# A Hyena block with a gated feed-forward on one core: three steps moved in ScalarE's instruction list

## What is computed

```python
u  = x @ in_proj_w.T + in_proj_b                  # 512 -> 3*512
uc = depthwise causal conv of 3 taps over u + short_b
x0, x1, v = split(uc)
v  = v * x1
v  = fftconv(v, k, filter_bias)                   # k: a 512-tap filter from a small sine network
y  = v * x0
x  = layernorm(x + y @ out_proj_w.T + out_proj_b)
gate = silu(x @ Wg.T); up = x @ Wu.T              # 512 -> 1408, quantised weights
x  = layernorm(x + (gate * up) @ Wd.T)
```

## Time and profile before

| | us |
|---|---|
| median of 3 runs | 1137.11 |
| lowest, highest | 1135.48, 1208.80 |
| the profiled execution, its own time | 1135.29 |
| its span, first to last instruction | 1133.5 |
| TensorE matmul busy | 1042.8 |
| VectorE, GpSimd, ScalarE busy | 794.9, 631.5, 463.3 |

### The profile page before, as it was taken

One profiled execution on the slowest core, in us unless ns is written; L12 is line 12 of the kernel. 1 busy time (PEld: TensorE's weight loads), 2 busy tenths in 40 slices (PEclk: granted clock), 3 DMA queues, 4 the chain that ended last, 5 costly groups with the idle time before them and its releaser, 6 DMA issues.

```text
span 1133.5 us, 18043 instructions
## 1 busy us (share of the span) xinstructions
PE 1042.8 (92%) x6378; PEld 839.7 (74%) x6378; DVE 794.9 (70%) x1455; ACT 463.3 (41%) x995; POOL 631.5 (56%) x677
## 2 busy tenths in 40 slices
PE   5896759999999999999999999999999999978996
PEld 3565647787887888788887888788887878867774
DVE  5666646687776878677787868677787878685443
ACT  3355524344444343444444444434444444423242
POOL 0147656557474657557475667557474657575211
PEclk9797979999999999999999999999999999999998
DMA  5245330222122221222222221222121221312332
GB/s 163 61 159 170 127 121 19 66 85 75 57 75 85 65 69 44 84 85 75 56 76 89 67 69 38 84 85 75 56 76 51 67 71 38 94 47 94 109 86 84
DMA packets 52215, 90.58 MB, mean 80 GB/s; under 512 B 6362, under 2 KB 11098, under 8 KB 52126
## 3 DMA queue, kind: packets, MB, share of 16 engines
q1 hardware_dynamic: 49072, 85.25, 24.8%
q10 hardware_dynamic: 3054, 4.18, 1.1%
HBM read 78.14 MB, written 11.27 MB: 79 GB/s over the span
## 4 chain that ended last, share of the span: by engine, by line
PE 73%; DVE 12%; ACT 5%; issue 5%; POOL 2%; DMA 2%; ACTq 0%; POOLq 0%; DVEq 0%
PE gate_up L884 10%; PE gate_up L885 10%; PE bank L756 10%; PE bank L758 10%; PE bank L757 10%; PE down L895 6%; PE down L896 6%; PE bank L847 2%; DVE hid_lo L746 2%; ACT hid L527 2%; DVE tmp L676 2%; PE spectrum L756 1%; PE spectrum L758 1%; PE spectrum L757 1%; PE bank L869 1%
## 5 line engine op out<-in xcount | busy, mean ns | idle before, releaser
L557 POOL TENSOR_TENSOR acc<-acc,tmp 128x256 f32<-128x256 f32 x160 | 124.3, 777 | 131.9 <-DVE tmp L676 121.2
L676 DVE TENSOR_TENSOR tmp<-spectrum,filt 128x512 f32<-128x512 f32 x256 | 173.1, 680 | 0.0
L756 PE MATMUL bank<-xT_hi,win_hi 128*128 128x512 f32 x384 | 162.9, 424 | 10.2 <-DVE cv L652 5.3
L884 PE MATMUL gate_up<-x2T_hi,wg_sb 128*128 128x256 f16 x704 | 167.4, 278 | 0.0
L885 PE MATMUL gate_up<-x2T_lo,wg_sb 128*128 128x256 f16 x704 | 165.4, 275 | 0.0
L884 PE MATMUL gate_up<-x2T_hi,wu_sb 128*128 128x256 f16 x704 | 163.7, 273 | 0.0
L885 PE MATMUL gate_up<-x2T_lo,wu_sb 128*128 128x256 f16 x704 | 163.5, 273 | 0.0
L895 PE MATMUL down<-wd_sb,hid_hi 128*128 128x512 f32 x352 | 148.9, 423 | 10.0 <-DVE hid_lo L746 5.3
L758 PE MATMUL bank<-xT_hi,win_lo 128*128 128x512 f32 x384 | 155.9, 406 | 0.0
L757 PE MATMUL bank<-xT_lo,win_hi 128*128 128x512 f32 x384 | 155.6, 405 | 0.0
L740 DVE SCALAR_TENSOR_TENSOR hid<-gate_up,up_scale,hid 128x256 f32<-128x256 f32 x176 | 84.5, 480 | 89.4 <-ACT hid L527 88.8
(11 more groups left out here) (110 smaller groups left out, 2161.1 us busy)
## 6 DMA issues: line engine op xcount, KB each, us to landing
wd_sb<-wd_scratch SPq DMA_DIRECT2D x176, 256.0 KB, 2.6
xstage<-in_x SPq DMA_DIRECT2D x32, 256.0 KB, 4.4
x<-in_x SPq DMA_DIRECT2D x32, 256.0 KB, 2.8
out<-x SPq DMA_DIRECT2D x32, 256.0 KB, 3.2
x<-in_win SPq DMA_DIRECT2D x12, 256.0 KB, 3.0
x2T_lo<-in_wd SPq DMA_DIRECT2D x6, 256.0 KB, 2.8
wd_scratch<-x2T_lo ACTq DMA_DIRECT2D x6, 256.0 KB, 2.1
x<-in_wd SPq DMA_DIRECT2D x5, 256.0 KB, 2.8
```

The source lines that it names most:

```text
L557: G.tensor_tensor(acc[:, i, 0, :], acc[:, i, 0, :], t[:, 1, :], ALU.subtract)
L676: TT(dst, spectrum[j % 2][:, :, :], k_part, ALU.mult).then_inc(made_done, 1)
L756: mm(out_ap, ah, bh, start=k == 0, stop=False)
L884: mm(dst, w[:, kb, rows(q)], x2T_hi[:, kb, ts], start=kb == 0, stop=False)
```

## The change

Three steps change their place in the list. The reader of `iv` is now called `y` and holds VectorE's three operations alone, at the old place. A step `z` with ScalarE's high part and GpSimd's low part stands right behind `silu` of the same beat. `norm` of the first layer norm moves from the tail of beat 9 to beat 10, behind `gu` and ahead of all other steps there. `psplit` of sum 3 moves from the tail of beat 9 to the tail of beat 10, behind `xsplit`.

```diff
-READER = {"ip": "conv", "iv": "z", "op": "ln1", "tv": "vsplit", "xt": "xsplit", "x2t": "x2split"}
+READER = {"ip": "conv", "iv": "y", "op": "ln1", "tv": "vsplit", "xt": "xsplit", "x2t": "x2split"}
@@ beat_steps
     earlier = shared(n, beat - 1) if beat else shared(n - 1, HB - 1)
+    if beat == 10 and out:
+        steps += [("norm", LN1, n - 2)]
     steps += readers([p for p in earlier if p[0] not in ("xt", "x2t")])
...
     if u:
         steps += [("silu", *u)]
+    steps += [("z", *at) for kind, *at in earlier if kind == "iv"]
...
-    if beat == 9 and out:
-        steps += [("norm", LN1, n - 2)]
     if beat in (9, 10):
         steps += readers([p for p in shared(n, beat) if p[0] == "xt"])
-    for i, ready in enumerate((1, 4, 7, 9)):
+    for i, ready in enumerate((1, 4, 7, 10)):
@@ build, VectorE's list
-                elif kind == "z":
+                elif kind == "y":
```

## The result

| | before | changed |
|---|---|---|
| median of the runs, us | 1137.8 | 1117.4 |
| lowest to highest | 1135.5 to 1208.8 | 1116.8 to 1119.1 |
| the profiled execution, its own time | 1135.3 | 1119.1 |
| its span | 1133.5 | 1117.3 |

The ratio is 0.9831 with a 95% interval of 0.9814 to 0.9849 (one disturbed run of before, the 1208.8, is left out of it): 1.7% less, just short of 2%, and 1115 had been forecast in a range of 1109 to 1123. The difference of the two medians is 20.4 us; by the ratio the saving is 19 us. The diff adds one line ahead of the engines' code, so L870 of the changed kernel is L869 of before, L641 is L640, and so on. The instructions are the same 18043.

A forecast was written before the change was run, and what follows sets the result against it. TensorE was taken as the bound from 200 to 990 us. Terms 10.8 + 5.2 + 1.2 + 3.2 = 20.4 us, off the profiled execution's 1135.3, gave 1114.9, said as 1115; range 1109 to 1123.

The forecast's parts named there:

- What bounds: From 200 to 990 us TensorE bounds; two of its waits, at transposes and down projection, carry 16.9 of 18.7 idle us.
- Activation before z, beat 9: Beat 9's product, high and low part come 0.95 us earlier; the even stages' down projection stalls go, 5.2 us.
- norm behind xsplit: Odd stages: the transposes' stall of 2.35 us goes, 0.56 returns at x2t; net 1.8 us each, 10.8 in six.
- Even and odd together: The period of an even and an odd stage together falls by 2.6 us.
- Stage 3's first Silu: Table load and activation run 1.4 us or more earlier, so a convolution starts sooner; 1.2 us saved (0 to 1.5).
- Clock: Slowdowns after the transposes' stall in two odd stages go, 3.2 us; no slice below 1.00 from 200 to 990 us.
- psplit of sum 3: Moved behind the second xsplit, its low part ends near 485, over 5 us before it is needed; effect nothing.
- Beats 2, 3 and 6: Earlier activation is worth nothing there; z behind it costs at most one activation, 0.47 us, on z.
- the tail holds no stall of these two kinds worth a term: After 990 us, no transposes' or down projection stalls large enough to count; no term in the sum.

The follow-up runs named there:

- activation_only: The changed kernel with norm and the split of sum 3 back at the end of beat 9; 1124.3 us, 0.989 of the kernel before.
- psplit_only: The kernel before with only the split of sum 3 moved to the tail of beat 10; 1136.4 us, ratio 1.000.
- norm_only: The kernel before with only norm moved to the head of beat 10; 1135.4 us, 0.999 of the kernel before.
- all_but_psplit: The changed kernel with the split of sum 3 back at the end of beat 9; 1123.1 us, 0.987 of the kernel before.

## Why the prediction was right, point by point

- **What bounds.** Right. In the middle of the kernel all that was gained lies in the two waits of the earlier trace rows; stage 3 adds 1.2 us.
- **Activation before z, beat 9.** Right: activation_only alone ends the down projection's stalls and shortens the transposes' by 0.73 us where 0.95 was expected: the low part was sized at 0.42 us and took 0.67, since it now meets GpSimd's low part of z. The signs named for it came: in the changed kernel the activation of beat 9 starts at 468.40 behind gate and up, and the product (L741) at 469.33 without a wait.
- **norm behind xsplit.** Right in the sum, and its timeline held to a tenth: L641 of block 2 was to end 4.30 us after the shift began (483.14 against 478.84) and ended some 4.2 us after it (475.63 and half of 1.29 against 472.08). `x2t`'s wait was put at 0.36 us and measured 0.46, and the 0.2 us within it came too (1.25 us for its eight matmuls in place of 1.04). But the move is not worth 1.8 us in each odd stage by itself: alone it gave back 1.8 of 2.2 us.
- **Even and odd together.** 2.6 us forecast for each pair, 2.4 measured (126.7 to 124.3).
- **Stage 3's first Silu.** 1.2 us forecast, 1.48 - 0.29 = 1.2 measured. A drain of 1.38 us on each switch, the figure of the Trainium skill (ScalarE: Activation LUTs, "What ACT_TABLE_LOAD costs") that would have brought this term near nothing, does not show at this load: before, it begins 0.02 us behind the copy ahead of it, and the activation follows 0.01 us behind the load.
- **Clock.** Right for the stalls it was about: no stretch of 10 us between 200 and 980 us is below 0.99 now; before there were two at 0.83. The sign was stated up to 990 us, and there it failed: stage 16's fall, at 1002.55 before, begins at 982.50 now. The size holds luck: the profiled execution of psplit_only, with the same six stalls, has one such fall in this stretch and not two.
- **psplit of sum 3.** "Nothing" was wrong. Its lateness did cost nothing, as said, but its old place would have cost 4.5 to 5.7 us. I had put the shift at 0.15 us without asking what runs on GpSimd at that moment. That the sum held is luck here: the shift took 0.14 us only because the change moved the split too. The trace of before showed the danger: the shift of the second layer norm (L723 too) takes 1.24 us in 13 of 16 cases, each time beside L551 on GpSimd.
- **Beats 2, 3 and 6.** The step that failed is "costs at most one activation (0.47 us) on z". z waits for as long as the activation does, until gate and up end: 2.5 us in stage 16. And "the tail holds no stall of these two kinds worth a term" looked only for stalls to be gained there, not for a chain through GpSimd that could grow. It cost 1.45 us. The other 1.4 us that the end lost in the profiled execution went with the clock.

The sum was 20.4 us. The profiled executions differ by 1135.3 - 1119.1 = 16.2. What is missing is the 2.8 us at the end, 0.9 us by which the changed kernel's execution was behind at 164 us (164.68 against 163.82), ahead of anything the change touches, and smaller terms. By the ratio of all runs the saving is 19 us. That the medians differ by the forecast 20.4 to the tenth is chance: the middle gave less than its terms, and the end lost.

## What to carry to other kernels

Move a step on an in-order engine only after writing down what the step that now stands ahead of it waits for, in the steady part and once more at either end, where other work no longer hides it: the wait moves with it. Parts of a reordering that share one chain can be worth little alone and more together: of two stages' 126.7 us the activation alone took 1.4, norm alone and the split alone nothing, the three together 2.4. So their single effects do not add up. And look at the tiny operations: a 2-element operation behind the wrong neighbour took as long as the rest of that neighbour's full tile, 1.03 us instead of 0.14, and cost 0.9 us in each two stages. A step of its own that took it out of the way gave 1.5 us there, more than the move of the split.

## What the runs showed of the hardware

VectorE's shift, two small operands in SBUF, took 0.14 to 0.16 us alone. In the odd stages of norm_only and all_but_psplit, where it began 0.15 to 0.26 us after GpSimd's 128x512 subtraction, it took 1.03 to 1.15 us and ended 0.01 to 0.02 us after it each time. In the even stages of all_but_psplit both began within 0.03 us of each other: three shifts took 1.27 to 1.29 us, the other four 0.15, and there it was GpSimd's operation that was longer (1.32 us instead of 1.28).

The Trainium skill (SBUF — State Buffer, "SBUF: two separate sides") says that VectorE operations with two SBUF inputs and GpSimd operations that read SBUF take a shared pair of ports in turn, each for a whole instruction. The traces agree. In the kernel before, VectorE's low part L746, with both operands in SBUF, took 0.41 to 0.43 us in the 111 cases in which GpSimd was idle at its start, and 1.11 (the median of 65) where GpSimd was busy; L676, whose spectrum comes from PSUM, took 0.68 in both cases. Two of them in a row in the changed kernel (990.05 to 991.67) show it at one place: L747 took 1.01 us instead of 0.42, and L677 its usual 0.68.

The granted clock fell after the waits of 2.2 us in two of six stages of the kernel before, and in the changed kernel not once behind waits of 0.46 us. Behind the stalls of 1.25 to 1.50 us of activation_only it did not fall either, and behind the 1.8 us of norm_only it fell once in six.
